# Packed table words for TensorE in a routed-expert stage, and the find work in other steps of the group

## The reference

```python
x = x + attn(layernorm(x))
y = layernorm(x)
scores = sigmoid(y @ w_router)                      # 64 experts
# best 4 of 8 groups of experts, then the best 8 experts in them
w = 2.5 * scores[top8] / sum(scores[top8])
# every (token, expert) pair, sorted by expert:
o = (silu(y @ we_gate[e]) * (y @ we_up[e])) @ we_down[e]   # 512 -> 256 -> 512
out = x + sum over the token's 8 experts of w * o + shared expert
```

## Time and profile before

| | |
|---|---|
| time, median of 3 runs (lowest, highest) | 3917.77 us (3917.01, 3926.54) |
| the profiled execution's own time | 3922.13 us |
| its span, first to last instruction | 3919.9 us |
| mean granted TensorE clock over the span | 0.969 |
| PE busy | 3590.6 us (92%) |
| PEld busy | 2851.5 us (73%) |
| DVE busy | 2350.7 us (60%) |
| ACT, POOL busy | 1387.9 us (35%), 1679.9 us (43%) |
| first expert tile's first gate product starts | 860.7 us |
| last expert tile's first gate product starts | 3875.7 us |

### The profile page before, as it was taken

How to read it: one execution, slowest core, us unless ns; L and a number is a source line. 1 busy time by engine, 2 the same in 40 slices (tenths; PEclk the granted TensorE clock), 3 DMA queues, 4 the chain that set the end, 5 groups by cost and what they waited for, 6 DMA issues and landing times.

```text
span 3919.9 us, 111436 instructions
## 1 busy us (share of the span) xinstructions
PE 3590.6 (92%) x17240; PEld 2851.5 (73%) x17241; DVE 2350.7 (60%) x5852; ACT 1387.9 (35%) x4097; POOL 1679.9 (43%) x1369
## 2 busy tenths in 40 slices
PE   6808999949999999999999899999999999999996
PEld 3406777738777778787878788787888877788785
DVE  5365767755566665666565665666555566566553
ACT  2213333313333433334333433333333344334331
POOL 1110111125455555455555454555554555555543
PEclk9958999969999999999999999999999999999998
DMA  3332333236666666666666666666666667667654
GB/s 114 105 65 94 114 102 112 90 73 126 155 136 138 153 152 135 142 146 159 126 138 127 171 124 140 130 146 138 124 132 132 140 153 162 142 124 162 129 102 73
DMA packets 216180, 502.43 MB, mean 128 GB/s; under 512 B 46587, under 2 KB 46715, under 8 KB 215360
## 3 DMA queue, kind: packets, MB, share of 16 engines
q0 software_dynamic: 129024, 320.94, 43.5%
q1 hardware_dynamic: 86592, 177.77, 13.8%
q10 hardware_dynamic: 512, 3.15, 0.4%
HBM read 1115.65 MB, written 191.41 MB: 333 GB/s over the span
## 4 chain that ended last, share of the span: by engine, by line
PE 59%; issue 5%; DVE 5%; DMA 3%; DVEq 3%; ACT 2%; ACTq 1%; POOLq 0%; POOL 0%; SPq 0%
PE e_ps_gu L1518 34%; PE e_ps_y L1537 16%; PE e_ps_x L1488 5%; DVE e_w_low L1660 3%; DMA out<-e_y,e_y_ids 3%; PE e_ps_h L1547 3%; ACT e_w_high L1597 1%; PE e_ps_find L1500 1%; DVEq L1382 1%; ACTq L1382 1%; DVE e_past L1692 1%; DVE e_y L1687 0%; DVE e_below L1703 0%; DVEq L1660 0%; DVEq L1663 0%
## 5 line engine op out<-in xcount | busy, mean ns | idle before, releaser
L1462 POOL DMA_INDIRECT out<-e_y,e_y_ids x576 | 951.3, 1651 | 1321.6 <-ACT e_weight L1609 601.8
L1518 PE MATMUL e_ps_gu<-e_w_high,e_xT_high 128*128 x2304 | 687.9, 418 | 14.2 <-issue 5.5
L1454 POOL DMA_INDIRECT e_x<-token_rows,e_x_ids x576 | 611.4, 1061 | 206.3 <-issue 173.1
L1518 PE MATMUL e_ps_gu<-e_w_low,e_xT_high 128*128 x2304 | 647.5, 400 | 6.2 <-issue 4.5
L1518 PE MATMUL e_ps_gu<-e_w_high,e_xT_low 128*128 x2304 | 651.4, 401 | 1.7 <-issue 1.6
L1687 DVE TENSOR_SCALAR e_y<-e_ps_y,e_weight 128x512 f32 (+1 forms) x576 | 431.0, 748 | 253.8 <-PE e_ps_y L1537 216.1
L1668 DVE TENSOR_TENSOR e_xT_low<-e_ps_x,e_xT_high 128x512 fp32r<-128x512 f32 x576 | 397.5, 690 | 265.2 <-ACT e_xT_high L1605 184.3
L1518 PEld LDWEIGHTS e_ps_gu<-e_w_high,e_xT_low 128*128 128x128 f32 x2304 | 430.3, 189 | 128.7 <-issue 28.9
L1518 PEld LDWEIGHTS e_ps_gu<-e_w_low,e_xT_high 128*128 128x128 f32 x2304 | 429.0, 188 | 126.9 <-issue 31.4
L1616 ACT ACTIVATE e_silu<-e_ps_gu 128x256 f32<-128x256 f32 x576 | 222.7, 387 | 828.5 <-PE e_ps_gu L1518 625.3
L1518 PEld LDWEIGHTS e_ps_gu<-e_w_high,e_xT_high 128*128 128x128 f32 x2304 | 396.0, 191 | 97.1 <-issue 35.9
(11 more groups left out here) (262 smaller groups left out, 4159.7 us busy)
## 6 DMA issues: line engine op xcount, KB each, us to landing
e_w_raw<-in_L_ffn_we_gate SPq DMA_DIRECT2D x576, 512.0 KB
e_w_raw<-in_L_ffn_we_up SPq DMA_DIRECT2D x576, 512.0 KB
e_w_raw<-in_L_ffn_we_down SPq DMA_DIRECT2D x576, 512.0 KB
a_x<-in_L_attn_x SPq DMA_DIRECT2D x64, 256.0 KB, 3.6
t_x_in<-in_L_attn_x SPq DMA_DIRECT2D x64, 256.0 KB, 2.8
token_rows<-t_xn SPq DMA_DIRECT2D x64, 256.0 KB, 2.1
out<-t_y_out SPq DMA_DIRECT2D x64, 256.0 KB, 2.1
e_x<-token_rows,e_x_ids POOLq DMA_INDIRECT x576
```

Source lines behind the costliest of these rows:

```text
L1454: pool.indirect_dma_start(x[:, s % XS, :], None, k.rows, bass.IndirectOffsetOnAxis(x_ids[:, s:s + 1], 0)) \
L1462: pool.indirect_dma_start(k.out, bass.IndirectOffsetOnAxis(y_ids[:, s:s + 1], 0), y[:, s % YS, :], None, compute_op=ALU.add).then_inc(adde ...
L1518: last = nc.tensor.matmul(ps_gu[s % 2][:], x[:, s % 2, c, :], w[:, c], start=(n == 0), stop=(n == 3 * DC - 1))
```

## The change

Each of PE's words now serves many tiles. `tile_table` also stores the slot and the expert of each tile as floats (`pairs`, a second small DRAM array), loads them back as one row and packs them on DVE, in chains of multiply-and-add with a drain between the links: the slots of eight tiles in one word (2 bits each) and the experts of four tiles in another (6 bits each), side by side in `k.packed`. The block ends when DVE has written them.

On PE, step 0 of eight reads the slot word before `turn_x`; `gate_up` and `down` shift and mask their slot out of it each time (`place_of`). The slot word of the eight tiles before is read once more in step 0, for the two `down` that reach back. The expert word is read in steps 0 and 4, and the four experts are cut out of it in the same step. Over eight tiles that is 4 reads.

`find` moves from step 3 to step 1 of the group, with the same position between `turn_x` and `gate_up`; both `pick` move to steps 2 and 3, for the group whose `find` was one step earlier; `mark` stays in step 2, behind the `pick`, and is for the group after. DVE's code ahead of the loop gets the third group's second `pick` and one more `mark`. The expert weight of a row goes to one of eight columns instead of four, at an address that both ACT and DVE compute, and ACT's wait for `scale` reaches back eight tiles instead of four. The other engines keep their own reads of `k.tiles`.

```diff
@@ tile_table, VectorE
+            nc.vector.tensor_copy(pairs[:, :, 0], place[:])
+            nc.vector.tensor_copy(pairs[:, :, 1], expert[:])
...
+            v.wait_ge(pairs_stored, 32)
+            for t in range(UNROLL - 2, 0, -1):
+                nc.vector.scalar_tensor_tensor(
+                    out=places[:], in0=by_eight[:, :, UNROLL - 1, 0] if t == UNROLL - 2 else places[:],
+                    scalar=float(WSLOTS), in1=by_eight[:, :, t, 0], op0=ALU.mult, op1=ALU.add)
+                if t >= SHORT:
+                    nc.vector.scalar_tensor_tensor(
+                        out=experts[:], in0=by_four[:, :, SHORT - 1, 1] if t == UNROLL - 2 else experts[:],
+                        scalar=float(E), in1=by_four[:, :, t - SHORT, 1], op0=ALU.mult, op1=ALU.add)
+                v.drain()
+            nc.vector.scalar_tensor_tensor(out=packed_eight[:, :, 0], in0=places[:], scalar=float(WSLOTS),
+                                           in1=by_eight[:, :, 0, 0], op0=ALU.mult, op1=ALU.add)
+            nc.vector.tensor_copy(packed_four[:, :, 1], experts[:])
@@ tile_table, SyncE
             sp.wait_ge(made, 1)
+            sp.dma_start(k.pairs.rearrange("(q p) f -> p q f", p=P), pairs[:]).then_inc(pairs_stored, 16)
             sp.dma_start(k.table.rearrange("(q p) f -> p q f", p=P), table[:]).then_inc(stored, 16)
+            sp.wait_ge(pairs_stored, 16)
+            sp.dma_start(pairs_row[:], k.pairs.unsqueeze(0)).then_inc(pairs_stored, 16)
             sp.wait_ge(stored, 16)
@@ expert_tiles, TensorE
-            words = Words(pe)
+            def packed(i, most):
+                return pe.value_load(k.packed[0:1, bass.ds(i, 1)], min_val=0, max_val=most)
+
+            def place_of(s):
+                return pe.snap((places[0 if s >= 0 else 1] // WSLOTS ** (s % UNROLL)) & (WSLOTS - 1))
...
-            def expert_of(i):
-                return pe.snap(entry(pe, i, 0, 2 * WSLOTS * E - 1) // (2 * WSLOTS), min_val=0, max_val=E - 1)
+            def expert_of(t):
+                return pe.snap((found_in[0] // E ** t) & (E - 1), min_val=0, max_val=E - 1)
...
-                place = words.place(s)
+                place = place_of(s)
...
-                if third == 1 and s + 1 < UNROLL:
-                    words.load(i + 1, s + 1)
-                if s == 0 and third == 0:
-                    words.load(i - 2, s - 2)
-                if s == 0 and third == 2:
-                    words.load(i - 1, s - 1)
-                if s % SHORT in (1, 2) and third != 1:
-                    t = 2 * (s % SHORT - 1) + third // 2
-                    if exists(i - s % SHORT + AHEAD_FIND + t):
-                        held[t] = expert_of(i - s % SHORT + AHEAD_FIND + t)
+                if s == 0 and third == 0 and exists(i - UNROLL):
+                    places[1] = packed(i - UNROLL, WSLOTS ** UNROLL - 1)
+                if not exists(i - s % SHORT + AHEAD_FIND):
+                    return
+                if s % SHORT == 0 and third == 0:
+                    found_in[0] = packed(i + AHEAD_FIND + 1, E ** SHORT - 1)
+                if s % SHORT == 0 and third > 0:
+                    for t in (2 * third - 2, 2 * third - 1):
+                        held[t] = expert_of(t)
 
             def step(i, s):
+                if s == 0:
+                    places[0] = packed(i, WSLOTS ** UNROLL - 1)
                 if exists(i + 1):
                     turn_x(i + 1, (s + 1) % UNROLL)
-                if s == 0:
-                    words.load(i, s)
-                if s % SHORT == SHORT - 1 and exists(i + 1 - SHORT + AHEAD_FIND):
-                    find(i + 1 - SHORT + AHEAD_FIND, held)
+                if s % SHORT == 1 and exists(i - 1 + AHEAD_FIND):
+                    find(i - 1 + AHEAD_FIND, held)
@@ expert_tiles, ScalarE (VectorE's scale reads the same column)
-                after(act, y_made, i - SHORT + 1)
-                nc.scalar.copy(weight[:, s % SHORT:s % SHORT + 1],
+                after(act, y_made, i - UNROLL + 1)
+                nc.scalar.copy(weight[:, bass.ds(slot, 1)],
@@ expert_tiles, VectorE
-                if s == 1 and exists(i - s - SHORT + AHEAD_FIND):
-                    pick(i - s - SHORT + AHEAD_FIND, 2)
-                if s == 2 and exists(i - s + AHEAD_FIND):
-                    mark(i - s + AHEAD_FIND)
-                if s == 3 and exists(i - s + AHEAD_FIND):
-                    pick(i - s + AHEAD_FIND, 0)
+                if s in (2, 3) and exists(i - s + AHEAD_FIND):
+                    pick(i - s + AHEAD_FIND, 2 * s - 4)
+                if s == 2 and exists(i - s + SHORT + AHEAD_FIND):
+                    mark(i - s + SHORT + AHEAD_FIND)
...
-                if i + SHORT < AHEAD_FIND:
-                    pick(i, 2)
+                pick(i, 2)
+            mark(AHEAD_FIND)
```

More of the change, by code:

```diff
@@ L1148, in tile_table @@
         table = sb("table", [P, Q, 3], I32)
+        pairs = sb("pairs", [P, Q, 2])
+        pairs_row = sb("pairs_row", [1, TABLE, 2])
+        places = sb("places", [1, TABLE // UNROLL])
+        experts = sb("experts", [1, TABLE // SHORT])
         ends = sb("ends", [E, 1])
@@ L1305, in expert_tiles @@
         x = sb("x", [P, XS, ROW])
-        weight = sb("weight", [P, SHORT])
+        weight = sb("weight", [P, UNROLL])
         xT_high = sb("xT_high", [P, 2, DC, P], F32R)
@@ L1574, in step @@
                 if exists(i - 2):
-                    down(i - 2, (s - 2) % UNROLL)
-            held = [None] * SHORT
+                    down(i - 2, s - 2)
             for i in range(0, AHEAD_FIND, SHORT):
-                find(i, [expert_of(i + t) for t in range(SHORT)])
+                found_in[0] = packed(i + 1, E ** SHORT - 1)
+                find(i, [expert_of(t) for t in range(SHORT)])
             turn_x(0, 0)
@@ L1687, in scale @@
                 nc.vector.tensor_scalar(y[:, bass.ds(slot, 1), :].rearrange("p o d -> p (o d)"), ps_y[s % 2][:],
-                                        weight[:, s % SHORT:s % SHORT + 1], None, ALU.mult).then_inc(y_made, 1)
+                                        weight[:, bass.ds(slot, 1)], None, ALU.mult).then_inc(y_made, 1)
             def mark(i):
@@ L1773, in program @@
         k.counts = nc.dram_tensor("rank_counts", [NB, E, P], BF16).ap()
+        k.pairs = nc.dram_tensor("tile_pairs", [(TILES // P + 1) * P, 2], F32).ap()
         k.table = nc.dram_tensor("tile_table", [(TILES // P + 1) * P, 3], I32).ap()
@@ L1782, in program @@
         k.tiles = sb("tiles", [1, TABLE * 3], I32)
+        k.packed = sb("packed", [1, TABLE], I32)
         with ExitStack() as early:
```

8 lines of the change are left out of this document (added).

## The result

The changed kernel takes 3881.19 us, the median of four runs (3878.34 to 3883.53), against 3918.61 of four runs of the kernel before. The ratio is 0.990, with a 95% interval of 0.9883 to 0.9917: some 37 us faster. The forecast was 3838. The profiled execution took 3878.34 us (span 3876.1 us, clock 0.969), 43.8 less than that of before.

What follows compares the result with a forecast made beforehand. PE's own stream bounds the kernel, losing 120 us against its undisturbed pace. Terms -41 - 43 + 0 + 3 + 0 + 1.5 = -79.5 us gave 3838 us from 3917.8; 8-in-10 range 3810 to 3884.

Steps and rivals of the forecast that it cites:

- mask a group ahead: `mark` three steps before its find removes PE's waits for DVE's mask: gain 41 us, at least 26, at most 45.
- fewer words: On PE's sequencer 18 table reads over eight tiles become 4: gain 43 us, bounds 20 and 58.
- weight columns: ACT's 209.6 us wait for `scale` goes, but PE never waited for it except through DVE: 0, bounds -5 and 0.
- order of find, pick, mark: DVE's step 2 fills up; PE may wait for `turn_h` at 16 expert changes, 11 us at most: +3 us.
- start: Table stage: 3 us of packing on DVE, partly offset by fewer reads before PE's first find: net +1.5 us, bounds 0 and +6.
- the 5.10 that the prediction set as its own test: The prediction is wrong if the steps do not come down to a mean near 5.10 us from 5.24.
- I let the gain be in proportion, 14/18: Of 58 us lost at PE's word reads, the share of reads removed, 14/18, is won: 45 us.
- against PE's 4.91: full, but not over: DVE's step 2, with a `pick` and the `mark`, takes 4.8 us and still fits PE's undisturbed step.
- The rival of DVE as the bound (B): DVE late in steps 2 and 3 at all 64 expert changes by some 1 us: 3902 us; chance 0.08.
- rival A: Reads were hidden anyway and issue gaps stay, so only the mask's wait goes: 3881 us; chance 0.13.
- The forecast's own mark for A: PEld's issue idle time in gate and up products, 96 us before, forecast under 30; above 60 the words step is wrong.
- queue of 64 entries: Skill's TensorE queue holds 32 weight-load and product pairs, over a step's 24, so reads would be worth nothing; prediction disagreed.

Runs made afterwards that it cites:

- mask alone: Kernel before with only `mark` moved to step 0 of the group, three steps ahead of its find: 3880.93 us, 0.9893.
- words and mask: Kernel before with packed words and `mark` in step 0; find in step 3, picks in steps 1 and 3, old weight columns: 3862.37 us, 0.9856.
- columns on words and mask: Kernel with packed words, find in step 3, picks in steps 1 and 3, mark in step 0, plus eight weight columns: 3862.13 us, 0.9856.
- the pick that was moved: Changed kernel with DVE's two picks in steps 1 and 3 instead of 2 and 3, mark still in step 2: 3866.47 us, 0.9852.
- words alone: Changed kernel with `find`, `pick`, `mark` and weight columns as before, so only the packed words are new: 3990.81 us, 1.0169.

## Why the prediction was wrong

In the order of its sum, with what the profiles of the kernels that carry each part show in its place (differences in the tiles):

| term | forecast | measured | from |
|---|---|---|---|
| mask a group ahead | -41 | -40.8 | mask alone against before |
| fewer words | -43 | -24.5 | words and mask against mask alone |
| weight columns | 0 | -2.3 | columns on words and mask |
| order of find, pick, mark | +3 | +20.1 | after against the one above |
| start | +1.5 | +5.3 | first gate product |

The four terms of the tiles make -47.5, which is the measured change because each kernel is compared with the next, so their sum confirms nothing; in another order they would be sized otherwise, as the columns show (-6 alone, -2 or nothing at the end). The mean step came down to 5.16 us, not to the 5.10 that the prediction set as its own test. Two terms failed by about the same amount, the words by 18 us and the order by 17, and the start by 4.

**The mask: right**, place and size. The forecast took the wait shown and added 0.46 us to each for what does not show. The 0.46 holds: the kernel's late finds take 0.84 us to the gate product, those in time 0.33. What it did not see is that such a wait can bring the clock down; before, with 10 us of the tiles at the lower level, the mean clock of the stage did not show it.

**The words: right in kind, too large.** The step that failed is "I let the gain be in proportion, 14/18". By the table of losses, the mask alone loses 54.2 us in steps 1, 2, 5 and 6, and words and mask lose 18.9 there: 35 us won from the 12 reads of these steps. (Steps 3 and 4 read one word each before, and step 7 none: with the four of step 0 these are the 18.) But step 0 went from 17.3 to 23.4 and steps 3, 4 and 7 from 8.8 to 12.5. Reads are not priced by number: 0.055 us each in one place and 0.29 in another. The three reads left in step 0 cost more there than the four of before: its first eight gate products lose some 11 us, against 3 with the mask alone, where I took off 2 for "two of them back to back". The rest of the shortfall is in steps 3, 4 and 7 and in what still stands in steps 1, 2, 5 and 6 without a read. How much of it is the new register work no run separates, but there is little of it: of the 3384 and 2304 register instructions in the gate products after, 2880 and 2304 stood there before, and the undisturbed step did not get longer. These are the rows of the kernel after, sequencers, ns min/median/max, against the earlier trace rows:

```profile
L1557 PEldq ALU_OP  x3384: 32/32/54, 865.4 to 3831.8; - x200
L1557 PEldq FUSED_REGOPS  x2304: 46/46/51, 865.5 to 3831.3; - x192
...
L1539 PEldq ALU_OP  x1015: 32/36/54, 848.5 to 3782.1; - x170
```

At the find it does show. Its line had no ALU instruction before and has 1015 now, and the four finds behind a late wait start 0.33 us apart in the start-up, 0.16 before.

**The order: the other step that failed.** Step 2 was put at 4.8 us "against PE's 4.91: full, but not over", and the price only for 16 of the 64 changes of expert, +3. Measured, it is 20 us. The sum checked only whether DVE gets through its steps, and whether `turn_h` waits; it had no term for what a late DVE does to `turn_x`, to the find and to the lead of PE's sequencer. The rival of DVE as the bound (B) named the mechanism, with 64 us given back, but not the place: step 4 loses between its last gate product and the next step's first, where `turn_x` and the find stand (27 of its 30 us), step 0 at the reads behind a short lead (27 of 35), and `turn_h` waits for only 3.3 us. B's argument against itself, "steps 0 and 1 have 1.8 us of slack each to catch up", is what the added work answers: this slack is in use, and 1 us taken from it in step 1 cost 30 us. So part of the order's price is where DVE's work falls, shown by the pick that was moved (9 to 15 us); the rest, 5 to 11 us, is `find` in step 1 and the mark in step 2, not taken apart further.

**The time 3881 was that of rival A**, by luck and not by its reason. A had the reads hidden in full and the issue gaps unchanged. The issue gaps halved, the words were worth 24.5 us, and the order and the start took 25 back. The forecast's own mark for A was gaps that stay above 60 us in PEld; they are 48.9, between A's mark and the forecast's 30.

**The Trainium skill's queue of 64 entries** ("TensorE: Matmul & The Clock Gate", Architectural detail), from which the prediction worked out that no read would reach the array, does not give the price here: 360 reads in quiet steps cost 20 us. But it points the right way, since only 0.055 of 0.75 us comes through there.

**The start**: the packing was priced a little low (4.1 us up to the mask, against 3). The step that failed is that the transfers would go as before: small stores and loads in flight together took 2.2 us more on the path, where 0.4 was counted. The saved reads show (1.0 us from the first mask to the first find instead of 3.0), but they bought nothing, since the path no longer goes over the find: ScalarE's first split, which in the prediction hung on it, now waits for the weights.

## What to carry to other kernels

Before working on a stream's small losses, look for the one instruction that others wait for just after it is made, and move it a group ahead: that alone was worth as much as the whole change. When a helper engine shows 60% busy, test its slack by adding work in the place in question, instead of subtracting means, and leave its work where it was already waiting for something. Packing words paid here by the reads that went; to spread those that remain gained next to nothing (1 and 2 us), and what made them dear was a late helper ahead of them. Try the parts in pairs, since one of them alone can make another's wait longer and the kernel slower than without either (0.9893 and 1.0169 alone, 0.9856 together).

## What the runs showed of the hardware

- A pause of PE of 1.53 us at a find, with the finds behind it issued slowly, was followed within about 2 us by a granted clock of 0.53 for 3 us; in the kernel with words alone, 30 such stretches took some 60 us more of full clock than the 3 of the kernel before. Pauses of 0.80 to 0.92 us were followed by it in 7 of 8 cases there and in none of 13 before, where the finds behind them issued faster.
- A register read of the table on PE's sequencer cost the time 0.055 us in a quiet step and 0.29 us behind two others, by runs with 360 and 72 added ones.
- About 1 us of work added to DVE in every fourth step, at 61% busy, cost 30 or 38 us in all over 144 times, by the step in which it stood; with the work in step 1, PE lost little in steps 1 and 2 and nearly all in steps 3 and 0.
- Two stores of 640 pieces, of 12 and of 8 bytes, in flight together on two queues, were seen as landed after 5.6 and 7.1 us, where the one of 12 bytes alone took 3.3; as the second one on one queue it took 6.4.
